# One straight list of steps over all head groups in place of a loop, and the first loads split over two queues

## The reference

```python
def attention(x, Wqkv_w, Wqkv_b, lambdas, subln_w, out_w, out_b):
    q, k, v = split(x @ Wqkv_w.T + Wqkv_b)        # q: 16 x 128, k: 8 x 128, v: 4 x 256
    ...                                           # k and v serve two query pairs each
    p1 = softmax(causal(q[..., 0, :] @ k[..., 0, :].T * D ** -0.5))
    p2 = softmax(causal(q[..., 1, :] @ k[..., 1, :].T * D ** -0.5))
    lam = exp(sum(lq1 * lk1)) - exp(sum(lq2 * lk2)) + LAMBDA_INIT
    o = (p1 - lam * p2) @ v
    o = o * rsqrt(mean(o * o) + EPS) * subln_w * (1.0 - LAMBDA_INIT)
    return o.reshape(B, S, H * D) @ out_w.T + out_b

def ffn(x, ...):
    x = fwht(x * SU_ug) / SCALE
    x = silu((x @ W_gate.T) * scales_gate) * ((x @ W_up.T) * scales_up)
    x = fwht(x * SU_dp) / SCALE
    return (x @ W_down.T) * scales_down
```

## Time and profile before

| | |
|---|---|
| runs | 1498.61, 1499.89, 1500.41 us, median 1499.89 |
| the profiled execution | 1500.61 us, its span 1498.8 us |
| mean granted TensorE clock | 0.973 |
| prologue, up to the first group's weight transposes | 0 to 23.65 us |
| first group | 23.65 to 345.26 us |
| second, third | 345.26 to 666.08 to 987.4 us |
| fourth | 987.4 to 1302.4 us |
| feed-forward part | 1302.4 to 1498.8 us |

### The profile page before, as it was taken

The page is one execution under the profiler, slowest core; times in us unless marked ns, Lnnn a source line. Parts: engine busy times, 40 slices in busy tenths (PEclk is TensorE's granted clock), DMA queues, the critical chain, the costliest instruction groups (busy, mean ns, idle before and its releaser), DMA issues. The chain is left out here.

```text
span 1498.8 us, 26747 instructions
## 1 busy us (share of the span) xinstructions
PE 1398.8 (93%) x8440; PEld 1237.8 (83%) x8440; DVE 1054.8 (70%) x2630; ACT 883.8 (59%) x2489; POOL 842.2 (56%) x1316
## 2 busy tenths in 40 slices
PE   5999999987999999979999999979999999669998
PEld 4889999877889999868899898768899898547887
DVE  6677787754777787736777887647777887585654
ACT  4566666654676667635667666536667666353331
POOL 1566665651766666634666666607666666434544
PEclk9999999998999999989999999989999999879999
DMA  5000000001000000010000000010000000130000
GB/s 144 8 2 1 1 2 1 1 2 45 8 1 1 1 1 1 1 44 9 2 1 1 2 1 1 1 45 8 1 1 1 2 1 1 28 114 1 11 15 32
DMA packets 25569, 20.46 MB, mean 14 GB/s; under 512 B 8896, under 2 KB 24128, under 8 KB 25408
## 3 DMA queue, kind: packets, MB, share of 16 engines
q1 hardware_dynamic: 25408, 18.52, 4.3%
HBM read 16.41 MB, written 2.10 MB: 12 GB/s over the span
## 5 line engine op out<-in xcount | busy, mean ns | idle before, releaser
L712 ACT ACTIVATE e<-score_bank,negmx 128x512 f32<-128x512 f32 (+2 forms) x640 | 394.3, 626 | 67.9 <-DVE negmx L815 67.2
L908 POOL TENSOR_TENSOR e<-e 128x512 f32<-128x512 f32 (+3 forms) x256 | 294.7, 1151 | 21.3
L628 PE MATMUL turn_bank<-v_hl,pT_hi 128*128 128x512 f32 x784 | 287.8, 402 | 5.5 <-DVE pT_lo L821 5.1
L606 PE MATMUL score_bank<-k_hi,q_hi 128*128 128x512 f32 (+2 forms) x640 | 258.5, 404 | 10.6 <-ACT e L712 9.6
L811 DVE TENSOR_REDUCE mx<-score_bank 128x1 f32<-128x512 f32 (+1 forms) x384 | 244.1, 637 | 26.6 <-PE score_bank L608 25.2
L608 PE MATMUL score_bank<-k_hi,q_lo 128*128 128x512 f32 (+2 forms) x640 | 232.9, 364 | 0.0
L607 PE MATMUL score_bank<-k_lo,q_hi 128*128 128x512 f32 (+2 forms) x640 | 232.8, 364 | 0.0
L892 POOL TENSOR_TENSOR inv_s<-s,neg_one 128x1 f32<-128x1 f32 x128 | 70.5, 551 | 283.7 <-DVE s L875 282.9
L630 PE MATMUL turn_bank<-v_hl,pT_lo 128*128 128x256 f32 x784 | 219.8, 280 | 0.0
L806 DVE CUSTOM_DVE_ANT_0 score_bank<-score_bank,mask 128x384 f32<-128x384 f32 (+3 forms) x256 | 143.5, 561 | 65.8 <-PE score_bank L608 64.5
L905 POOL TENSOR_SCALAR e<-e,ratio 128x512 f32<-128x512 f32 (+3 forms) x256 | 177.6, 694 | 12.2
(11 more groups left out here) (299 smaller groups left out, 3558.9 us busy)
## 6 DMA issues: line engine op xcount, KB each, us to landing
w_raw<-in_L_attn_Wqkv_w_dram SPq DMA_DIRECT2D x5, 512.0 KB, 3.5
w_raw<-in_L_attn_Wqkv_w_dram SPq DMA_DIRECT2D x10, 256.0 KB, 3.8
x_in<-_attn_hidden_states_dram SPq DMA_DIRECT2D x4, 512.0 KB, 5.9
e<-in_L_attn_out_w_dram SPq DMA_DIRECT2D x4, 512.0 KB, 4.2
out_dram<-d_out SPq DMA_DIRECT2D x16, 128.0 KB, 1.7
x_res<-_attn_hidden_states_dram SPq DMA_DIRECT2D x1, 1536.0 KB, 12.6
bv<-in_L_attn_Wqkv_b_dram SPq DMA_DIRECT2D x10, 128.0 KB, 4.1
raw<-in_L_ffn_W_up_dram SPq DMA_DIRECT2D x2, 512.0 KB, 6.2
```

Source lines behind the costliest of these rows:

```text
L606: pe.matmul(bank[:, 0:w], qh, kh, start=True, stop=False)
L628: pe.matmul(bank[:, :], pT_hi[:, q % PT_SLOTS, b * P:(b + 1) * P], v_hl[:, kt, :], start=(kt == 0), stop=False)
L712: act.activation(e, S[k % NS][:, 0:w], ACT.Exp, bias=negmx[:, d % 2, m, s:s + 1], accum_out=ssum[:, d % 4, s, m, c:c + 1]).then_inc(s_act, 1)
L908: pool.tensor_tensor(a, a, b, ALU.add).then_inc(p_pool, 1)
```

## The change

- `attention_steps()` makes one list of 1761 steps for all four groups, without a loop, and the prologue's work is in the list too: LN (statistics), NX (normalize), X (transpose and split of tokens), LAM, WQ and WK (splits of weights).
- The projections of the next group's keys come in the last half of one group (TURN_OF_GROUP[31]) and in the first of the next (TURN_OF_GROUP[0]), its values at the end of the third half and in the fourth (2 and 3). WQ and WK of the next group are steps at the end of halves 27 and 28, WO follows the last OP of the group before. HEAD replaces FIRST_HALVES for the first group.
- The host lays weights out already transposed, so no weight is transposed on TensorE. WQ and WK are one instruction of 1024 elements on ScalarE and one on VectorE each, out of SBUF. Bias columns of all groups are loaded once.
- The bias addition of a value unit is two instructions of 256 columns; it goes to v_sum, a tile of its own, and no longer to slots of e1.
- The first half of a duo has one more T before its P.
- acc is no longer filled: the first visit of a tile adds to the bias row.
- SyncE asks for the tokens except tiles 2 and 3, then lambdas and bias rows; ScalarE's queue asks for tiles 2 and 3, for all weights of group 0 in one transfer of 1 MB and for the bias columns.
- SBUF tensors lie at addresses written out; the scratch of dynamic DMA is 1024 bytes.

```diff
-HALVES = ('TSSTSSPTSoQTPPPTO', 'TSTSSOSTPSoQTPPTP')
-FIRST_HALVES = ('KQSKKKSVSVSSVVVVV', 'SVWSWSQSS')
+HALVES = ('TSSTSSTPTSoQTPPPTO', 'TSTSSOSTPSoQTPPTP')
+HEAD = {0: 'SKSKSKQSKS', 1: 'SVSVSQVSVS', 2: 'SVSVSQSVSV', 3: 'TSTSSOSTPSoQTPPTP'}
+TURN_OF_GROUP = {0: 'TSSTKSSTPKTSoKQTPPKPTO', 2: 'TSSTSSTPTSoQTPPPTOVV', 3: 'VTVSVTVSSOVSTVPSoQTPPTP',
+                 27: 'TSTSSOSTPSoQTPPTPw', 28: 'TSSTSSTPTSoQTPPPTOk', 31: 'TSKTSSKOSTPKSoQTPKPTP'}
...
-SCALAR_LAGS = {'K': 1, 'V': 1, 'QP': 0, 'OP': 0}
-VECTOR_LAGS = {'PV': 1, 'T': 1, 'OT': 1, 'W': 1, 'K': 1, 'V': 1}
+SCALAR_LAGS = {'K': 1, 'V': 1, 'X': 1, 'QP': 0, 'OP': 0}
+VECTOR_LAGS = {'PV': 1, 'T': 1, 'OT': 1, 'WO': 1, 'K': 1, 'V': 1, 'X': 1}
...
+    for kind, what in (("LN", 0), ("LN", 1), ("NX", 0), ("X", 0), ("X", 1), ("WK", 0), ("LN", 2), ("NX", 1),
+                       ("K", (0, 0, 0)), ("X", 2), ("X", 3), ("WQ", 0), ("LN", 3), ("NX", 2),
+                       ("K", (0, 0, 1)), ("X", 4), ("X", 5), ("QP", (0, 1, 0)), ("NX", 3), ("K", (0, 0, 2)),
+                       ("X", 6), ("X", 7), ("QP", (0, 0, 0)), ("LAM", None), ("K", (0, 0, 3)), ("QP", (0, 0, 1)),
+                       ("QP", (0, 1, 1))):
+        emit(kind, what)
...
-                nc.all_engine_barrier(sems_to_clear=range(sems[0].num, sems[-1].num + 1))
...
+            @block.sync
+            def _(sp):
+                sp.dma_start(x_in[:, 0:2, :], x_tiles[:, 0:2, :]).then_inc(x_landed[0], 16)
+                for q in range(1, 4):
+                    sp.dma_start(x_in[:, 4 * q:4 * q + 4, :], x_tiles[:, 4 * q:4 * q + 4, :])\
+                      .then_inc(x_landed[q], 16)
+                sp.dma_start(lam_in[:, :, :], lams.rearrange("(a k) d -> a k d", a=1).broadcast_to([P, 4, D]))\
+                  .then_inc(lam_landed, 16)
...
+                for g in range(GROUPS):
+                    if g > 0:
+                        sp.wait_ge(w_lo, w_use["WO", (g - 1, 1)] + 1)
+                        sp.dma_start(w_raw[:, :, :], w_qkv[g]).then_inc(w_landed, 16)
+                    sp.wait_ge(w_lo, max(w_use["WQ", g], w_use["WK", g]) + 1)
+                    sp.dma_start(w_raw[:, 0, :], w_o[g]).then_inc(w_landed, 16)
...
+                act.dma_start(x_in[:, 2:4, :], x_tiles[:, 2:4, :]).then_inc(x_landed[0], 16)
+                act.dma_start(w_raw[:, :, :], w_qkv[0]).then_inc(w_landed, 16)
+                act.dma_start(col[:, :], cols[:, :]).then_inc(cols_landed, 16)
...
+                    elif kind == "WQ":
+                        act.wait_ge(w_landed, 16 * (2 * what + 1))
+                        if what > 0:
+                            act.wait_ge(r_full, r_use["QP", (DUOS // 2 * what - 1, 1, 1)] + 1)
+                        act.activation(wq_hi[:, :, :], w_raw[:, :, 0:BANK], ACT.Copy, scale=SCALE).then_inc(w_hi, 1)
...
+                        dve.wait_ge(w_hi, w_use[kind, what] + 1)
+                        dve.scalar_tensor_tensor(out=wq_lo[:, :, :], in0=w_raw[:, :, 0:BANK], scalar=SCALE,
+                                                 in1=wq_hi[:, :, :].bitcast(F32), op0=ALU.mult,
+                                                 op1=ALU.subtract).then_inc(w_lo, 1)
...
-    nc = _bacc.Bacc("TRN2", target_bir_lowering=False, num_devices=1)
+    nc = _bacc.Bacc("TRN2", target_bir_lowering=False, num_devices=1, dynamic_dma_scratch_size=1024)
```

More of the change, by code:

```diff
@@ L43 @@
 DUOS = TILES
+ALL_DUOS = GROUPS * DUOS
 CHUNKS = 5
@@ L134, in emit @@
             to_project.append(what)
+        if kind == "OP" and what % (2 * DUOS) == 2 * DUOS - 1 and what // (2 * DUOS) + 1 < GROUPS:
+            for s in range(2):
+                emit("WO", (what // (2 * DUOS) + 1, s))
     def pv_part(h):
         db = (h - 3) // 2 if h % 2 else (h - 4) // 2
-        if not 0 <= db < DUOS:
+        if not 0 <= db < ALL_DUOS:
             return []
@@ L160, in attention_steps @@
             else:
-                queue = {"T": turns, "S": scores, "P": products, "Q": extra, **setup}[what]
+                queue = {"T": turns, "S": scores, "P": products, "Q": extra, "K": keys, "V": values,
+                         "w": split_q, "k": split_k}[what]
                 if queue:
                     emit(*queue.pop(0))
-        for what in (*turns, *scores, *products):
+        if h == 2:
+            for s in range(2):
+                emit("WO", (0, s))
+        for what in (*turns, *scores, *products, *keys, *extra):
             emit(*what)
-        assert h == 0 or not any(setup.values())
+        del keys[:]
+        if at == 3:
+            assert not values
     while exps_due or factors_due or mixes_due:
@@ L438, in build @@
                     n_qp[what] = len(n_qp)
+                if kind in ("K", "V"):
+                    kv_use[kind, what] = len(kv_use)
+                if kind == "V":
+                    n_v[what] = len(n_v)
+                if kind in ("WQ", "WK", "WO"):
+                    w_use[kind, what] = len(w_use)
+                if kind == "OP":
+                    tile = next(ch[2] for ch in duo_chunks(what // 2) if ch[0] == what)
+                    first_visit[what] = tile not in seen
+                    seen.add(tile)
             WORK = (T[0], T[1], R, O)
[L442 to L443 removed]
+            latest = [(-4, None), (-3, None), (-2, None), (-1, None)]
             bank_of, before = {}, {}
@@ L448, in build @@
                     use = ("PV", duo_chunks(what[0])[what[1]][0])
-                if kind in ("S", "END"):
+                if kind not in ("T", "PV", "OT", "OP", "QP", "K", "V"):
                     continue
                 if use not in bank_of:
-                    b = min(range(4), key=lambda b: last_use[b][0])
-                    bank_of[use], before[use] = b, last_use[b][1]
+                    b = min(range(4), key=lambda b: latest[b][0])
+                    bank_of[use], before[use] = b, latest[b][1]
                 held = kind == "PV" and not duo_chunks(what[0])[what[1]][5]
-                last_use[bank_of[use]] = (len(steps) if held else n, use)
+                latest[bank_of[use]] = (len(steps) if held else n, use)
             pool_mixed, dve_mixed = [], []
-            for q in range(CHUNKS * DUOS):
+            for q in range(CHUNKS * ALL_DUOS):
                 on_dve = q % CHUNKS in DVE_MIXES
```

1158 lines of the change are left out of this document (550 added, 608 removed).

## The result

The changed kernel takes 1446.62 us (median of four executions, 1445.48 to 1450.26) against 1499.25 for the kernel before, a ratio of 0.9653 [0.9634, 0.9673]. Its profiled execution took 1450.26 us with a span of 1448.5. The forecast was 1433, the range 1419 to 1449: the sign and most of the size came as forecast, the point was 13.6 us too low. The median lies in the range, the profiled execution 1.3 us above it.

What follows compares the result with a forecast made beforehand. TensorE, busy 93% of the span, was taken as the bound, with gains only at group ends. Three boundaries at 24.3 - 3.0 (63.9 us) plus 3.2 at the head gave 67.1 off 1500.61: forecast 1433 us, range 1419 to 1449.

Steps and rivals of the forecast that it cites:

- gross 24.3 us a boundary: Between head groups: the most a boundary can give, present period 320.86 us against 296.6 packed, before new costs.
- price list: Per-step TensorE prices (0.235 us per 512 columns, 0.118 per 256, 0.11 per transpose), giving 296.6 us for a packed group.
- WO ... bounded by 0 and 2.45 in the same way: At each boundary: output-weight splitting on ScalarE and VectorE costs TensorE between 0 and 2.45 us; 0.5 taken.
- Edits at nothing: Edits priced at zero, among them the extra T before P, the split value addition, bias columns and fixed addresses.
- land at about 7.0: Head: weights on a second queue delay the second token block to about 7.0 us, 1.1 after VectorE finishes the first's statistics.
- the stall of 2.0: Head, first score to output-tile transpose number 4: 2.0 us of stall taken, between 0 and 5.6, beside 74.9 of work.
- 38.4 + 80.5, gain 0: Head's lower bound: first score at 38.4 us, then 80.5 to transpose number 4, stalls as now, gaining nothing.
- Packed: Rival: no new stall, slack covers all, 79.1 us gained, 1421 us; chance 0.13.
- Bursts bite: Rival: weight splits delay maxima and exponentials in full, 9 us a boundary, nothing at the head, 1454 us; chance 0.17.
- the drain and refill stay: Rival at the boundaries: only barrier and weight transposes go, 32.4 us gained, 1467 us; chance 0.05.
- The slower rival: Rival: the reordered first half makes TensorE wait for a split once per duo, 82.6 us lost, 1515 us; chance 0.03.
- wrong would be: Signs against the forecast: a middle slower than 17.03 us a duo, a period over 305, or a first score after 42.

Runs made afterwards that it cites:

- e8b_short_splits: Changed kernel with the query and key weight splits (WQ, WK) of groups 1 to 3 written for 8 columns instead of 512: 1439.93 us, one execution.
- e2_short_wo: Changed kernel with the output-weight split of groups 1 to 3 written for 8 columns instead of 256: ratio 0.9654 to the kernel before.
- e9b_old_first_half: Changed kernel with the first half's old order, without the extra T before the first P: ratio 0.9658 to the kernel before.
- e5_wo_order: Changed kernel with the output-weight half needed first split first, each output projection waiting only for its own half: ratio 0.9667 to the kernel before.
- the repeat: The changed kernel run again with no edit: median 1446.64 us, ratio 0.9673 to the kernel before.
- e3_values_first: Changed kernel with the first group's eight value units put among the first scores, before the first mixes: ratio 0.9684 to the kernel before.
- e11b_best: Changed kernel with one queue for first loads, output weights split and waited for by halves, WQ and WK of groups 1 to 3 in two pieces each: 1440.65 us.
- the order turned: Changed kernel, two queues, with VectorE normalizing the first token block before taking the second's statistics: ratio 0.9654 to the kernel before.
- e4_wo0_later: Changed kernel with the first group's output-weight split one half later, after half 3 instead of half 2: ratio 0.9653 to the kernel before.
- e10b_double_turns: Kernel before with each of a group's 16 query, key and value weight transposes made twice: 1505.28 us against 1497.87 for the kernel before beside it.

## Why the prediction was right, and where its sizes were off

- **What bounds it: right.** Attention is TensorE's own work outside the boundaries; after the change the pair 20 to 22 still takes 17.05 (before 17.07), numbers 4 to 22 take 152.67 (before 153.04), and the granted clock stays at 1.00 from 125 to 1250 us.
- **The gross 24.3 us a boundary: right as far as it can be read.** The kernel with the least weight work (e8b_short_splits) has a period of 300.1; with the 1.3 of the output weights (e2_short_wo) and the 0.45 of the extra T (e9b_old_first_half) taken off as well, 298.3 is left by subtraction, beside 296.6 of the price list. The 1.7 between them was not taken apart: it can be the key and value units, what the shortened instructions still take, or the list's own error, which exists, since the list misses about 0.5 us for numbers 0 to 2, where nothing is added (16.88 after, 16.86 before).
- **The terms that come in their place: mis-sized.** Period 302.24 instead of 299.6, 5.6 of cost instead of 3.0:

| term | forecast | measured by its removal |
|---|---|---|
| WQ | 1.0 | 0.92 |
| WK | 1.0 | 1.30 |
| WO | 0.5 | 1.3 |
| extra T before P | 0 | 0.45 |
| values and what no run took apart | 0.5 | 1.7 |

The largest miss with a name is "WO ... bounded by 0 and 2.45 in the same way" with 0.5 taken. The slack of VectorE in the middle (78%) was the wrong row for it: WO stands in front of what TensorE takes next, the new group's first output projection and the split of the probabilities queued behind it (e5_wo_order), and there the mean slack says nothing. A larger part, the 1.2 between 0.5 and 1.7 in the last line, stays open. Over three boundaries the shortfall is 8.0 us. The extra T was in "Edits at nothing"; it is 0.45 a boundary, given back in part at the end.

- **The head: the sign was wrong, by 12.0 us in the profiled execution and 8.9 in the repeat.** Three steps failed. First, "land at about 7.0": the second block landed at 8.7, and with VectorE's order the chain behind it moved by the whole lateness. Between kernels with a like clock that is 2.9 us (39.33 in e3_values_first, 36.47 in e11b_best) or 3.3 (42.32 in the changed kernel, 39.03 with one queue), where the forecast had 1.0. Second, the stall of 2.0 from the first score on: the waits are 4.4 to 4.7. Third, no term at all for the clock. It cost 3.0 us before the first score (42.32 against 39.33 with the same order and queues) and 4.2 behind it: the earlier trace rows was read as a wait of 1.98 us, and not as one behind which the granted clock drops, to 0.66 over 65 to 70 us in the kernel before and to 0.57 and 0.50 over 75 to 85 us here. The chain itself was priced about 0.9 too long (37.4 forecast without lateness, 36.47 measured in e11b_best). So the 39.03 with one queue and the 38.79 with the order turned look like the forecast's 38.4 by luck: they hold a low clock that the forecast left out and a chain shorter than it had. The bound "38.4 + 80.5, gain 0" did not hold the loss.
- **The ends: not in the sum, +3.2 us.** Number 100 to 127 is 1.3 shorter, of which the extra T gives 0.9. From number 127 to the first feed-forward transpose it takes 12.10 instead of 14.21: SyncE issues its first load for this part 3.9 us after number 127 instead of 5.2. Which edit does it was not tried.
- **The sum again:** 1433.5 + 8.0 + 12.0 - 3.2 = 1450.3, the profiled execution's 1450.26; with the repeat's head and ends, 1433.5 + 8.3 + 8.9 - 4.1 = 1446.6. That the median lies inside the range is luck in part: without the 3.2 to 4.1 us of the ends, which the forecast did not have, it would stand at 1450 to 1451, and the bound that the range set on the head did not hold.
- **The rivals.** Packed fell: every weight split shows. Bursts bite, with 9 us a boundary, fell in its size; 5.6 lies between it and the forecast, its mechanism is the one seen. That the drain and refill stay (1467) fell with the period: 302.24, where it would have left 310. The slower rival fell with e9b_old_first_half.
- **The signs for it.** Under "wrong would be" stood a period over 305 (302.2, held), a first score after 42 (42.32 in the first execution, 41.43 in the repeat), which flagged the head rightly, and a middle slower than 17.03 a duo. Numbers 4 to 24 take 170.91, 17.09 a duo, so by its letter that sign came too. It was set over the wrong stretch: 22 to 24 now holds the split of WQ (18.24, before 17.28), and without that pair the middle is no slower. The stalls came at WQ, WK and WO as forecast, but the trace puts them down to pT_lo and wo_lo, not to exponentials or maxima.

## What to carry to other kernels

Work that an added instruction brings to an engine with slack on average still cost TensorE here about the length of one engine's instruction (0.92 and 1.30 us for 1.08 and 1.23) where it stood in front of what TensorE takes next; price it by that neighbour and not by the busy share, and cut it into pieces placed apart (0.9 of 2.2 us came back here). A wait that was moved came back a few us later (e5_wo_order, e4_wo0_later); at the boundaries work taken away or spread returned far more time than work moved. Before a second queue is given to large weights, ask which small transfer behind the first is next on the chain, and which order of the engine's work would do without it for longest.

## What the runs showed of the hardware

- In a sparse stretch a wait costs more than its length: behind 1.94 us of waiting at 75 us the granted clock was 0.57 and 0.50 over the next ten us in one execution, 0.72 and 1.00 in another of the same kernel. The head up to number 4 differs by 3.1 us between these two profiled executions, and the end by 1.1. The changed kernel took 1445.5 to 1446.7 us in the six executions with a mean granted clock of 0.984 or 0.985 and 1450.3 to 1451.6 in the three with 0.981 or 0.982.
- The moment at which the granted clock comes back moves the first score of the same order by 3.0 us (42.32 and 39.33) and by 2.6 (39.03 and 36.47).
- Weight transposes start 0.21 us apart at the lower level (1.2 GHz) and 0.11 apart at the upper; in e10b_double_turns they began at the lower one after an idle gap of 5.4 us.
- For a split out of SBUF ScalarE takes 1.08 us with 1024 columns and 0.64 with 512 (e11b_best), VectorE 1.23 and 0.69: one long instruction is 16% and 11% cheaper than two, and at these boundaries two short ones placed apart were still better.
